# Gated scan and expert FFN kernel: the last second products by pairs of tiles, the last turned y over two banks, copies and turned states on finer signals

## The chip, the cores and the metric

The kernel runs on one core of one Trainium2 chip. The metric is the device time in microseconds (us) of one execution, as the median of several runs. Engines are TensorE (PE in the profile), VectorE (DVE), ScalarE (ACT), GpSimd (POOL) and SyncE (SP), which here only issues the DMAs.

## The reference, cut to what matters

Two sequences (batches) of 2048 tokens, 256 channels, all in f32. Every batch passes a recurrent layer and then a feed-forward layer, each between layer norms and added to what came in:

```
x = x + layernorm(attn(layernorm(x)))        # 512 inner channels, 32 heads of 16
x = x + layernorm(ffn(layernorm(x)))         # 2 of 8 experts, 1024 wide
# attn, for every token t, head by head, a state of two components S0, S1:
#   r0 = A11 S0 + A12 S1 ;  r1 = -A12 S0 + A11 S1
#   err = v - sum(k * r) ;  S = r + beta * err * k ;  y = sum(Q * S)
#   y = groupnorm(y, 32 groups, over tokens and channels of the group)
#   y = y * silu(z) + D * u ;  residual + y @ out_W.T
# ffn: pooled = mean of tokens; the best two experts by pooled @ Wr, weights by softmax
#   h = gelu(x @ W1[e] + b1[e]) ;  out = sum over the two e of w[e] * (h @ W2[e] + b2[e])
```

## The kernel before, in words

The code is written by hand for each engine as one program in order, with counting semaphores between them. No scheduler moves anything.

**Tiling.** The 2048 tokens of a batch are 128 chunks of 16 (L = 16). Partition c holds chunk c, and tile j holds token j of every chunk, so one step over j works on all chunks at once. The recurrence runs in two passes. `pass_1` finds for each chunk the map from its first state to its last. `chunk_scan` joins the 128 maps: VectorE multiplies the three parts of each component o by the end factors (L1733, L1734, `end_ready`), TensorE turns the results over (L624, `end_turned`), ScalarE copies the six turned parts into `mts` (L1030, `mt_ready`), VectorE scans them by small products (L1753 to L1774, `scan_done`), TensorE turns the chunks' first states back (L634, `start_ready`). `mts` lies where the first products of VectorE still read `PSt` (both are `work[0:3072]`), so that a copy may only begin when these are read.

**Pass 2** goes over j again: VectorE copies the turned states (L1798), rotates the queries of a tile by its coefficients (`turn`, L1784, after TensorE's query of L654), and does the updates of L1806 to L1825. After a tile, TensorE turns y_j into channel order (`turn_y`, L645, bank 6 or 7 of PSUM by j % 2), and ScalarE copies it out with its sum and squares it with its sum (L1047, L1052). After the last one VectorE takes the group sums (L1832), and the first gate (L1870) waits for the first normed y of ScalarE (L1082) and for x, which SP reloads once VectorE has finished the last tile.

**Experts.** Each batch's FFN has 64 units (NF). A unit is `up`, four instructions of 128x512 (L767) into bank 4 or 5, a gelu by ScalarE (L1158), and `down`, eight instructions of 128x256 (L781) that add to four token tiles in banks 6 and 7. 16 units complete a block of four tiles (two experts by eight). The FFN of batch 0 is spread through batch 1's recurrence in the code. That of batch 1 stands alone at the end. There the order on TensorE is up(i), down(i-1). Weights come by pairs of units into a ring of four pairs (`load_pairs`, L386 and L388), and pair p is issued when `down` of pair p-4 is finished. Behind the last pair in SP's queue stand the four stores of the result (L478). `last_norm` on VectorE takes each block: bias (L1992), statistics (L1272), moments (L1278 to L1284), with ScalarE's root (L1173), then scales (L2001), normed tiles (L2006) and sums with x1 (L2010).

The functions that the change touches, with the line numbers of the profile:

## Time and profile before

| what | value |
|---|---|
| median of 3 runs | 1417.45 us (1414.99 to 1418.44) |
| the profiled execution, its own time | 1417.05 us |
| its span | 1415.1 us |
| TensorE busy | 1248.4 us (88%) |
| VectorE busy | 1126.5 us (80%) |
| ScalarE busy | 794.4 us (56%) |
| GpSimd busy | 174.0 us (12%) |
| mean granted TensorE clock | 0.958 |

The span goes from the first to the last instruction of the profiled execution, and its own time lies 1.95 us above it. Busy shares are averages over stages that have different limits, so they do not tell which engine sets the end in a stage: in the recurrence VectorE is nearly always at work, in the last FFN TensorE is. The kernel writes two results to memory. The last of them leaves in four stores of 512 KB, and the span ends with the last one's landing.

### The profile page before, as it was taken

To read this page: it belongs to the slowest core of one execution; us is meant where nothing else is said; L and a number is where in the kernel's file an instruction comes from. 1 tells how busy PE (TensorE), PEld (TensorE's weight loads), DVE (VectorE), ACT (ScalarE), POOL (GpSimd) and SP (SyncE) were. 2 spreads that over 40 slices of the span, in tenths; PEclk is the share of its full clock that TensorE was granted. 3 is DMA by queue.
4 is the path that set the end of the run, shared out by engine and by line. 5 is a ranking of instruction groups with operands and counts; after the bars stand their busy time and mean duration, and the time that the engine had idled before them with its cause. 6 is when DMAs were issued, how large, how long until landed. Compare 5 with 4: busy or idle time off the path is not lost. (4 is left out here: it accounts for less than half of the span.)

```text
span 1415.1 us, 14617 instructions
## 1 busy us (share of the span) xinstructions
PE 1248.4 (88%) x4248; PEld 737.3 (52%) x4248; DVE 1126.5 (80%) x1826; ACT 794.4 (56%) x2713; POOL 174.0 (12%) x77
## 2 busy tenths in 40 slices
PE   5987788863999879798999999899998898999997
PEld 3553333332555446465565555555554565666664
DVE  5989999998999979789899999889999793411011
ACT  4896566623788866858322323347888565333232
POOL 0000155410122200000011111002221000000000
PEclk9999899986999999899999999999999898999999
DMA  6004111010311022501223131313110106232221
GB/s 238 1 8 179 60 57 48 30 59 1 119 45 60 30 110 83 223 23 45 89 90 104 61 104 60 104 60 119 56 49 31 60 1 219 74 135 75 75 75 74
DMA packets 54400, 110.88 MB, mean 78 GB/s; under 512 B 4785, under 2 KB 40114, under 8 KB 52274
## 3 DMA queue, kind: packets, MB, share of 16 engines
q1 hardware_dynamic: 54322, 109.97, 21.9%
q8 instruction: 34, 0.56, 0.2%
q14 instruction: 44, 0.36, 0.1%
HBM read 81.64 MB, written 28.31 MB: 78 GB/s over the span
## 5 line engine op out<-in xcount | busy, mean ns | idle before, releaser
L781 PE MATMUL ps<-kz 128*128 128x256 f32 x1024 | 243.5, 381 | 13.5 <-ACT kz L1158 8.8
L781 PEld LDWEIGHTS ps<-kz 128*128 128x128 f32 x1024 | 194.3, 191 | 97.0 <-issue 63.0
L767 PE MATMUL ps<-kz 128*128 128x512 f32 x512 | 241.0, 594 | 0.3 <-DVE small L1980 0.3
L1158 ACT ACTIVATE kz<-ps,small 128x512 f32<-128x512 f32 x128 | 87.7, 686 | 272.3 <-PE ps L767 272.1
L654 PE MATMUL ps<-wshare,uT 128*128 128x512 f32 x512 | 229.0, 601 | 5.3 <-DVE work L1784 5.2
L654 PEld LDWEIGHTS ps<-wshare,uT 128*128 128x128 f32 x512 | 96.2, 193 | 117.9 <-issue 109.4
L568 PE MATMUL ps<-wshare,xnT 128*128 128x512 f32 x256 | 120.8, 616 | 32.4 <-ACT ps L862 32.4
L1005 ACT ACTIVATE work<-ps,coef 128x16 f32<-128x16 f32 x736 | 124.4, 388 | 35.5 <-DVE work L1774 26.9
L1223 POOL TENSOR_TENSOR work<-work 128x1024 f32<-128x1024 f32 x28 | 66.9, 2391 | 582.7 <-DVE work L1692 354.6
L767 PEld LDWEIGHTS ps<-kz 128*128 128x128 f32 x512 | 97.2, 191 | 76.3 <-issue 70.2
L1992 DVE TENSOR_TENSOR kz<-ps,b_s 128x256 f32<-128x256 f32 x16 | 6.3, 414 | 135.9 <-PE ps L781 135.9
L1240 POOL TENSOR_TENSOR kz<-work 128x1024 f32<-128x1024 f32 x30 | 71.6, 2385 | 278.5 <-DVE work L1813 278.5
L568 PEld LDWEIGHTS ps<-wshare,xnT 128*128 128x128 f32 x256 | 47.7, 196 | 85.9 <-issue 48.7
L862 ACT ACTIVATE ps<-bk_s 128x1024 f32<-128x1024 f32 x32 | 32.9, 1029 | 101.5 <-DVE wshare L1600 101.5
L1005 ACT ACTIVATE wshare<-ps,coef 128x16 f32<-128x16 f32 x512 | 86.8, 405 | 2.0 <-DVE work L1823 2.0
L548 PE MATMUL ps<-wshare,uT 128*128 128x352 f32 x256 | 78.1, 467 | 4.5 <-ACT uT L936 2.8
L645 PEld LDWEIGHTS ps<-ident,kz 128*128 128x128 f32 x512 | 65.3, 201 | 27.7 <-DVE kz L1795 18.0
L645 PE MATMUL ps<-ident,kz 128*128 128x128 f32 x512 | 66.7, 286 | 10.7 <-DVE kz L1795 10.7
L1784 DVE TENSOR_TENSOR work<-ps,coef 128x1024 f32<-128x1024 f32 x60 | 70.5, 1218 | 1.4 <-PE ps L654 1.4
L716 PE MATMUL ps<-wo_s,work 128*128 128x256 f32 x256 | 61.0, 401 | 6.5 <-DVE work L1257 6.5
L548 PEld LDWEIGHTS ps<-wshare,uT 128*128 128x128 f32 x256 | 49.3, 194 | 33.2 <-issue 7.6
L693 PE MATMUL ps<-xnT,wz_s 128*128 128x512 f32 x128 | 60.1, 616 | 2.1 <-DVE work L1784 1.9
(293 smaller groups left out, 2099.6 us busy)
## 6 DMA issues: line engine op xcount, KB each, us to landing
kz<-in_w SPq DMA_DIRECT2D x128, 256.0 KB, 3.0
kap_d<-kz SPq DMA_DIRECT2D x26, 512.0 KB, 2.7
kz<-kap_d SPq DMA_DIRECT2D x26, 512.0 KB, 3.3
kz<-in_x SPq DMA_DIRECT2D x3, 2048.0 KB, 8.3
v_d<-kz SPq DMA_DIRECT2D x4, 1024.0 KB, 4.5
wshare<-in_wq SPq DMA_DIRECT2D x2, 2048.0 KB, 8.0
coef<-in_x SPq DMA_DIRECT2D x2, 2048.0 KB, 8.1
work<-v_d SPq DMA_DIRECT2D x3, 1024.0 KB, 7.5
```

The costliest lines, as they stand in the source:

```text
L548: t = mm(ps[:, sm_bank(b, j), 0:NSM * H], uT3[:, k, j * P:(j + 1) * P], wsm_s[:, k, :], start=(k == 0), stop=(k == KI - 1))
L568: t = mm(ps[:, k_bank(b, i) + c, :], xnT[:, k, j * P:(j + 1) * P], wk_s[:, k, c, :], start=False, stop=(k == KM - 1), skip_group_check=True)
L645: t = mm(ps[:, 6 + j % 2, g * P:(g + 1) * P], qb(j)[:, i, g * P:(g + 1) * P], ident[:], start=(i == 0), stop=(i == 1))
L654: t = mm(ps[:, 2 * (j % 2) + c, :], uT3[:, k, j * P:(j + 1) * P], wq_s[:, k, c, :], start=(k == 0), stop=(k == KI - 1))
L716: t = mm(ps[:, 4 + j % 4, 0:DM], y2(n)[:, g, q * P:(q + 1) * P], wo_s[:, g, :], start=(g == 0), stop=(g == KI - 1))
L767: t = mm(ps[:, 4 + i % 2, :], w1_r[r][:, k, (f % 2) * P:(f % 2 + 1) * P], x2T[:, k, n * 512:(n + 1) * 512], start=(k == 0), stop=(k == KM ...
L781: t = mm(ps[:, 6 + q // 2, (q % 2) * DM:(q % 2 + 1) * DM], hbuf(i)[:, q * P:(q + 1) * P], w2_r[r][:, f % 2, :], start=(f == 0 and q % 2 == ...
L1005: t = af(dst[:, h * HD:(h + 1) * HD], src[:, h * HD:(h + 1) * HD], ACT.Copy, scale=c[:, h:h + 1])
L1158: af(hbuf(i), ps[:, 4 + i % 2, :], ACT.Gelu, bias=b1_s[:, f // FT, f % FT:f % FT + 1]).then_inc(h_done, 1)
L1223: nc.gpsimd.tensor_tensor(PSt[:, :, 2], PSt[:, :, 2], Z, ALU.add).then_inc(sum_ready, 1)
L1240: nc.gpsimd.tensor_tensor(qb(j), w[0], w[1], ALU.add).then_inc(turned_ready, 1)
L1784: t = tt(w, q, wide(cf[:, H_ + i:H_ + i + 3:2, j]), MUL)
```

## The change

It does five things.

- **Last eight units by pairs of tiles.** In batch 1's FFN, the `up` of units 56 to 63 follow each other. Then come the `down` of all eight for the first two tiles (bank 6, `pair_done` 1), and of all eight for the last two (bank 7, `pair_done` 2). The gelus of the last four units go to `wshare`.
- **The last block's norm** is done by two tiles at a time (`last_block`). ScalarE norms three of the four tiles in place of VectorE. The last store is cut into two of 256 KB.
- **The last turned y** (j = 15) of each batch is written to banks 6 and 7, two groups in each, with a signal after the first two (`first_half`).
- **The scan's copies** wait for `parts_used` (after VectorE's product for o = 1, a = 0) for the first three, and for the second `end_ready` for the last three.
- **Batch 1's turned chunk states**: TensorE turns them after the first half of query 0 instead of after the whole, and VectorE rotates query 0 by halves, the first ahead of the state copy (`turn_half`).

```diff
@@ -294,6 +301,9 @@
+        def y_bank(j, g):
+            return 6 + (g // 2 if j == L - 1 else j % 2)
         def sm_bank(b, j):
@@ -313,7 +323,9 @@
-        def hbuf(i):
+        def hbuf(b, i):
+            if b == B - 1 and i >= NF - 4:
+                return wshare[:, (i - NF + 4) * 512:(i - NF + 5) * 512]
             return hid[:, (i % 4) * 512:(i % 4 + 1) * 512]
@@ -473,11 +485,12 @@
             load_pairs(B - 1, chosen, 14, NF // 2)
-            for n in range(NCH):
-                sp.wait_ge(out_ready, B - 1 + 4 * n + 4)
-                sp.dma_start(out[B - 1].rearrange("(c j) d -> c j d", j=L)[:, 4 * n:4 * n + 4], x1_tok[:, 4 * n:4 * n + 4]
+            stores = [(4 * n, 4 * n + 4) for n in range(NCH - 1)] + [(L - 4, L - 2), (L - 2, L)]
+            for r0, r1 in stores:
+                sp.wait_ge(out_ready, B - 1 + r1)
+                sp.dma_start(out[B - 1].rearrange("(c j) d -> c j d", j=L)[:, r0:r1], x1_tok[:, r0:r1]
                              ).then_inc(out_stored, 16)
-            sp.wait_ge(out_stored, 16 * (B - 1 + NCH))
+            sp.wait_ge(out_stored, 16 * (B - 1 + len(stores)))
@@ -636,24 +649,31 @@
                 pe.wait_ge(yp_ready, b * L + j + 1)
-                if j >= 2:
+                if j == L - 1:
+                    pe.wait_ge(yt_done, b * L + j)
+                elif j >= 2:
                     pe.wait_ge(yt_done, b * L + j - 1)
...
                 for g in range(KI):
+                    if j == L - 1 and g == 2:
+                        t.then_inc(first_half, 1)
                     for i in range(2):
-                        t = mm(ps[:, 6 + j % 2, g * P:(g + 1) * P], qb(j)[:, i, g * P:(g + 1) * P], ident[:],
+                        t = mm(ps[:, y_bank(j, g), g * P:(g + 1) * P], qb(j)[:, i, g * P:(g + 1) * P], ident[:],
                                start=(i == 0), stop=(i == 1))
                 t.then_inc(yt_ready, 1)
+            def query_part(j, c):
+                for k in range(KI):
+                    t = mm(ps[:, 2 * (j % 2) + c, :], uT3[:, k, j * P:(j + 1) * P], wq_s[:, k, c, :],
+                           start=(k == 0), stop=(k == KI - 1))
+                return t
...
                     pe.wait_ge(kq_used, 2 * L * b + L + j - 1)
-                for c in range(2):
-                    for k in range(KI):
-                        t = mm(ps[:, 2 * (j % 2) + c, :], uT3[:, k, j * P:(j + 1) * P], wq_s[:, k, c, :],
-                               start=(k == 0), stop=(k == KI - 1))
-                t.then_inc(kq_ready, 1)
+                query_part(j, 0)
+                query_part(j, 1).then_inc(kq_ready, 1)
@@ -666,10 +686,12 @@
                         token_u(b, L + j, j)
-                    if b > 0 or j > 2:
+                    if b > 0 and j == 0:
+                        query_part(0, 0).then_inc(half_query, 1)
+                        turn_starts(b)
+                        query_part(0, 1).then_inc(kq_ready, 1)
+                    elif b > 0 or j > 2:
                         query(b, j)
-                    if b > 0 and j == 0:
-                        turn_starts(b)
                     if j >= 3:
@@ -778,17 +800,31 @@
                     for q in range(4):
-                        t = mm(ps[:, 6 + q // 2, (q % 2) * DM:(q % 2 + 1) * DM], hbuf(i)[:, q * P:(q + 1) * P],
+                        t = mm(ps[:, 6 + q // 2, (q % 2) * DM:(q % 2 + 1) * DM], hbuf(b, i)[:, q * P:(q + 1) * P],
                                w2_r[r][:, f % 2, :], start=(f == 0 and q % 2 == 0), stop=(f == 2 * FT - 1),
+                def last_downs():
+                    for a in range(2):
+                        for i in range(NF - HELD, NF):
+                            r, f = i // 2 % WR, i % (2 * FT)
+                            if a == 0:
+                                pe.wait_ge(h_done, b * NF + i + 1)
+                                pe.wait_ge(w2s_ready, b * (NF // 2) + i // 2 + 1)
+                            for q in (2 * a, 2 * a + 1):
+                                t = mm(ps[:, 6 + a, (q % 2) * DM:(q % 2 + 1) * DM], hbuf(b, i)[:, q * P:(q + 1) * P],
+                                       w2_r[r][:, f % 2, :], start=False, stop=(i == NF - 1), skip_group_check=True)
+                        t.then_inc(pair_done, 1)
                 for i in range(first, last):
                     up(i)
-                    if i >= 1:
+                    if i >= 1 and (b < B - 1 or i <= NF - HELD):
                         down(i - 1)
-                if last == NF:
+                if last == NF and b < B - 1:
                     down(NF - 1)
+                elif last == NF:
+                    last_downs()
@@ -1023,8 +1059,10 @@
-                act.wait_ge(end_ready, b * 2 + 2)
+                act.wait_ge(parts_used, b + 1)
                 for o in range(2):
+                    if o:
+                        act.wait_ge(end_ready, b * 2 + 2)
                     for i in range(3):
@@ -1042,13 +1080,18 @@
                         silu(b, 6)
-                    act.wait_ge(yt_ready, b * L + j + 1)
+                    if j == L - 1:
+                        act.wait_ge(first_half, b + 1)
+                    else:
+                        act.wait_ge(yt_ready, b * L + j + 1)
                     for g in range(KI):
-                        t = af(y_tok[:, j, g * P:(g + 1) * P], ps[:, 6 + j % 2, g * P:(g + 1) * P], ACT.Copy,
+                        if j == L - 1 and g == 2:
+                            act.wait_ge(yt_ready, b * L + j + 1)
+                        t = af(y_tok[:, j, g * P:(g + 1) * P], ps[:, y_bank(j, g), g * P:(g + 1) * P], ACT.Copy,
                                accum_out=gs[:, g, 0, j:j + 1])
...
                     for g in range(KI):
-                        y = ps[:, 6 + j % 2, g * P:(g + 1) * P]
+                        y = ps[:, y_bank(j, g), g * P:(g + 1) * P]
                         t = af(y, y, ACT.Square, accum_out=gs[:, g, 1, j:j + 1])
@@ -1153,9 +1196,9 @@
                     act.wait_ge(h_ready, b * NF + i + 1)
-                    if i >= 4:
+                    if 4 <= i < NF - 4 or (i >= 4 and b < B - 1):
                         act.wait_ge(d_done, b * NF + i - 3)
-                    af(hbuf(i), ps[:, 4 + i % 2, :], ACT.Gelu, bias=b1_s[:, f // FT, f % FT:f % FT + 1]
+                    af(hbuf(b, i), ps[:, 4 + i % 2, :], ACT.Gelu, bias=b1_s[:, f // FT, f % FT:f % FT + 1]
                        ).then_inc(h_done, 1)
@@ -1166,7 +1209,14 @@
                 elif last == NF:
-                    block_root(NCH - 1)
+                    for a in range(2):
+                        r = slice(L - 4 + 2 * a, L - 2 + 2 * a)
+                        act.wait_ge(fin_vec, B + NCH - 1 + a)
+                        af(t1[:, r], mv[:, r, 1], ACT.Sqrt, bias=eps5).then_inc(fin_act, 1)
+                        act.wait_ge(fin_scale, a + 1)
+                        for j in range(L - 4 + 3 * a, L - 2 + 2 * a):
+                            t = af(r_tok[:, j], r_tok[:, j], ACT.Identity, scale=rs2[:, j:j + 1], bias=nb[:, j:j + 1])
+                        t.then_inc(fin_normed, 1)
@@ -1730,7 +1780,12 @@
                     for a in range(2):
-                        link(tt(by_head(X[:, a], 1), by_head(PSt[:, a], 1), wide(ef[:, o, a]), MUL))
+                        t = tt(by_head(X[:, a], 1), by_head(PSt[:, a], 1), wide(ef[:, o, a]), MUL)
+                        if o == 1 and a == 0:
+                            t.then_inc(parts_used, 1)
+                            dve.wait_ge(parts_used, b + 1)
+                        else:
+                            link(t)
                     tt(X[:, 0], X[:, 0], X[:, 1], ADD).then_inc(end_ready, 1)
@@ -1784,6 +1839,12 @@
+            def turn_half(b, c):
+                for i in range(2):
+                    t = tt(by_head(q_parts(b, 0)[i][:, c * DI:(c + 1) * DI], 0), by_head(ps[:, c, :], 0),
+                           wide(cf[:, H_ + i + 2 * c, 0]), MUL)
+                return t
             def pass_2(b):
@@ -1794,10 +1855,14 @@
+                if b > 0:
+                    dve.wait_ge(half_query, b)
+                    turn_half(b, 0)
                 dve.wait_ge(start_ready, b + 1)
...
                 if b > 0:
-                    turn(b, 0)
+                    dve.wait_ge(kq_ready, 2 * L * b + L + 1)
+                    turn_half(b, 1).then_inc(kq_used, 1)
                 dve.wait_ge(start_used, b + 1)
@@ -2008,6 +2073,42 @@
                             tt(x1_tok[:, j], r_tok[:, j], x1_tok[:, j], ADD).then_inc(out_ready, 1)
+            def last_block(b):
+                b2c = b2_s[:, 0]
+                def sums(a):
+                    dve.wait_ge(pair_done, a + 1)
+                    for q in (2 * a, 2 * a + 1):
+                        tt(r_tok[:, L - 4 + q], ps[:, 6 + a, (q % 2) * DM:(q % 2 + 1) * DM], b2c, ADD).then_inc(fd_used, 1)
+                    for q in (2 * a, 2 * a + 1):
+                        dve.wait_ge(fd_used, L - 4 + q + 1)
+                        seen = stats(L - 4 + q, r_tok[:, L - 4 + q])
+                    moments(seen, slice(L - 4 + 2 * a, L - 2 + 2 * a)).then_inc(fin_vec, 1)
+                def scales(a):
+                    r = slice(L - 4 + 2 * a, L - 2 + 2 * a)
+                    dve.wait_ge(fin_vec, b + NCH + a)
+                    dve.wait_ge(fin_act, b + NCH + a)
+                    link(v.reciprocal(rs2[:, r], t1[:, r]))
+                    stt(nb[:, r], mv[:, r, 0], -1.0, rs2[:, r], MUL, MUL).then_inc(fin_scale, 1)
+                def result(j):
+                    tt(x1_tok[:, j], r_tok[:, j], x1_tok[:, j], ADD).then_inc(out_ready, 1)
+                sums(0)
+                scales(0)
+                sums(1)
+                dve.wait_ge(fin_normed, 1)
+                result(L - 4)
+                result(L - 3)
+                scales(1)
+                dve.wait_ge(fin_scale, 2)
+                t = mark(tsc(r_tok[:, L - 2], r_tok[:, L - 2], rs2[:, L - 2:L - 1], nb[:, L - 2:L - 1], MUL, ADD))
+                after(t)
+                result(L - 2)
+                dve.wait_ge(fin_normed, 2)
+                result(L - 1)
```

**ScalarE at batch 1's scan.** L1030 (after: L1068) are the six copies. L1158 (after: L1201) are the gelus around them. Before:

```order
L1154 ACTIVATE kz<-kz,small 128x512 [waits w_loaded0]
L1158 ACTIVATE kz<-ps,small 128x512 [waits d_done,h_ready]
L1030 ACTIVATE work<-ps 128x64x8 [waits end_turned,end_ready]
L1030 ACTIVATE work<-ps 128x64x8 [waits end_turned] x5
L1158 ACTIVATE kz<-ps,small 128x512 [waits d_done,h_ready]
L1154 ACTIVATE kz<-kz,small 128x512 [waits w_loaded1]
```

The first copy waited for the second `end_ready`, and with it all six and the gelu behind them. Of the change:

```order
L1197 ACTIVATE kz<-kz,small 128x512 [waits w_loaded0]
L1201 ACTIVATE kz<-ps,small 128x512 [waits d_done,h_ready]
L1068 ACTIVATE work<-ps 128x64x8 [waits end_turned,parts_used]
L1068 ACTIVATE work<-ps 128x64x8 [waits end_turned] x2
L1068 ACTIVATE work<-ps 128x64x8 [waits end_turned,end_ready]
L1068 ACTIVATE work<-ps 128x64x8 [waits end_turned] x2
L1201 ACTIVATE kz<-ps,small 128x512 [waits d_done,h_ready]
```

The order is the same. Only the wait for the second `end_ready` has moved from the first copy to the fourth.

**TensorE at the end of the program.** L767 (after: L789) is `up`, L781 is `down` (after: L816 in the held part). Before:

```order
L767 MATMUL ps<-kz 128x512 [waits h_done,w_loaded3]
L767 MATMUL ps<-kz 128x512
L781 MATMUL ps<-kz 128x256 [waits w2s_ready,h_done]
L781 MATMUL ps<-kz 128x256 x3
L781 MATMUL ps<-kz 128x256 [waits w2s_ready,h_done]
L781 MATMUL ps<-kz 128x256 x3
L43 UNCONDITIONAL_BRANCH
```

All four tiles got their last products in the last rows. Of the change, from the last `up` (the last `down` for the first pair of tiles and all of the second pair):

```order
L789 MATMUL ps<-kz 128x512 [waits h_done,w_loaded3]
L789 MATMUL ps<-kz 128x512
L816 MATMUL ps<-kz 128x256 [waits w2s_ready,h_done]
L816 MATMUL ps<-kz 128x256
```
```order
L816 MATMUL ps<-kz,wshare 128x256 [waits w2s_ready,h_done]
L816 MATMUL ps<-kz,wshare 128x256
L816 MATMUL ps<-kz 128x256 x8
L816 MATMUL ps<-kz,wshare 128x256 x8
L44 UNCONDITIONAL_BRANCH
```

The eight `down` of two products each for the first pair have their waits. The sixteen products of the second pair (x8 and x8) stand behind them and wait for nothing.

**VectorE at the end of the program**, from the last moments. Before:

```order
L1257 SCALAR_TENSOR_TENSOR small<-small 128x4 [waits vec_chain]
L2001 RECIPROCAL small<-small 128x4 [waits fin_act,fin_vec]
L1257 SCALAR_TENSOR_TENSOR small<-small 128x4 [waits vec_chain]
L2006 TENSOR_SCALAR kz<-kz,small 128x256 [waits vec_chain]
L2006 TENSOR_SCALAR kz<-kz,small 128x256
L2010 TENSOR_TENSOR coef<-kz,coef 128x256 [waits vec_chain]
L2006 TENSOR_SCALAR kz<-kz,small 128x256
L2010 TENSOR_TENSOR coef<-kz,coef 128x256 [waits vec_chain]
L2006 TENSOR_SCALAR kz<-kz,small 128x256
L2010 TENSOR_TENSOR coef<-kz,coef 128x256 [waits vec_chain] x2
```

Of the change:

```order
L2083 TENSOR_TENSOR kz<-ps,b_s 128x256 [waits pair_done]
L2083 TENSOR_TENSOR kz<-ps,b_s 128x256
L1322 BN_STATS small<-kz 128x6 [waits fd_used] x2
```
```order
L1307 SCALAR_TENSOR_TENSOR small<-small 128x2 [waits vec_chain]
L2097 TENSOR_TENSOR coef<-kz,coef 128x256 [waits fin_normed]
L2097 TENSOR_TENSOR coef<-kz,coef 128x256
L2093 RECIPROCAL small<-small 128x2 [waits fin_act,fin_vec]
L1307 SCALAR_TENSOR_TENSOR small<-small 128x2 [waits vec_chain]
L2107 TENSOR_SCALAR kz<-kz,small 128x256 [waits fin_scale]
L2097 TENSOR_TENSOR coef<-kz,coef 128x256 [waits vec_chain]
L2097 TENSOR_TENSOR coef<-kz,coef 128x256 [waits fin_normed]
```

After the last product there are two tiles of bias and statistics instead of four, and one tile normed by VectorE instead of four. The sums of the first pair of tiles stand ahead of the last reciprocal.

## Rows read from the trace of the kernel before

**Rows 1.** Busy time by stretch: us of PE, PEld, DVE, ACT, POOL, then PEclk, DMA share, GB/s.
```profile
965.00:1095.00 130.00, 122.43 (x472) 70.01 (x470) 128.18 (x133) 113.77 (x660) 30.62 (x13) 0.99 0.19 65
1186.00:1405.00 219.00, 217.32 (x759) 143.59 (x758) 42.66 (x146) 75.01 (x107) 0.00 (x0) 1.00 0.31 108
```

**Rows 2.** Timeline (start, us, engine, line, operation), batch 1's scan: DVE, ACT, PE.
```profile
901.67 3.55 DVE L1733 TENSOR_TENSOR work<-work,endf 128x1536 f32<-128x1536 f32 x2
912.51 1.03 DVE L1753 TENSOR_TENSOR work<-work 128x384 f32<-128x384 f32 x2 [5.17 <-ACT work L1030]
907.05 5.43 ACT L1030 ACTIVATE work<-ps 128x512 f32<-128x512 f32 x6 [8.07 <-DVE work L1734]
...
907.07 0.65 PE L624 MATMUL ps<-ident,work 128*128 128x128 f32 x4 [0.34 <-DVE work L1734]
912.99 1.99 PE L781 MATMUL ps<-kz 128*128 128x256 f32 x8 [1.58 <-ACT kz L1158]
```

**Rows 3.** Timeline, batch 1's first queries and turned states: PE, then DVE.
```profile
934.20 7.03 PE L654 MATMUL ps<-wshare,uT 128*128 128x512 f32 x16
941.07 1.04 PE L634 MATMUL ps<-ident,work 128*128 128x128 f32 x8
942.38 7.03 PE L654 MATMUL ps<-wshare,uT 128*128 128x512 f32 x16
...
935.37 1.78 DVE L1774 TENSOR_TENSOR work<-work 128x896 f32<-128x896 f32 x1
942.14 1.23 DVE L1798 COPY work<-ps 128x1024 f32<-128x1024 f32 x1 [4.08 <-PE ps L634]
949.45 2.36 DVE L1784 TENSOR_TENSOR work<-ps,coef 128x1024 f32<-128x1024 f32 x2 [1.36 <-PE ps L654]
```

**Rows 4.** Timeline of DVE at batch 0's scan.
```profile
308.43 3.55 DVE L1733 TENSOR_TENSOR work<-work,endf 128x1536 f32<-128x1536 f32 x2
...
314.08 4.62 DVE L1784 TENSOR_TENSOR kz<-ps,coef 128x1024 f32<-128x1024 f32 x4
319.30 1.03 DVE L1753 TENSOR_TENSOR work<-work 128x384 f32<-128x384 f32 x2 [0.61 <-ACT work L1030]
```

**Rows 5.** Timeline, last turned y: PE, ACT (third copy), DVE of batch 1; DVE of batch 0.
```profile
1105.23 1.95 PE L645 MATMUL ps<-ident,kz 128*128 128x128 f32 x16
...
1107.74 0.28 ACT L1047 ACTIVATE kz<-ps 128x128 f32<-128x128 f32 x1
...
1113.34 1.33 DVE L1870 TENSOR_TENSOR work<-kz,wshare 128x512 f32<-128x512 f32 x2 [0.95 <-ACT kz L1082]
...
513.77 1.29 DVE L1870 TENSOR_TENSOR work<-kz,wshare 128x512 f32<-128x512 f32 x2 [1.06 <-DMA coef<-in_x]
```

**Rows 6.** Timeline of the end, with SP's queue (SPq), and the last stretch by engine.
```profile
1380.24 32.23 SPq L478 DMA_DIRECT2D out<-coef  x4
1401.48 3.62 PE L781 MATMUL ps<-kz 128*128 128x256 f32 x16
1405.14 0.76 DVE L1992 TENSOR_TENSOR kz<-ps,b_s 128x256 f32<-128x256 f32 x2 [39.24 <-PE ps L781]
1408.57 0.30 ACT L1173 ACTIVATE small<-small 128x4 f32<-128x4 f32 x1 [4.90 <-DVE small L1257]
1411.35 0.76 DVE L2010 TENSOR_TENSOR coef<-kz,coef 128x256 f32<-128x256 f32 x2
...
1413.00:1414.00 1.00, 0.00 (x0) 0.00 (x0) 0.00 (x0) 0.00 (x0) 0.00 (x0) 0.50 0.98 401
```

**Rows 7.** Line L388, second weight load of a pair: issue to landing over all 64.
```profile
DMA to landing us min/median/max: 2.8/3.0/10.9
```

**Rows 8.** Timeline of PE, the output product of two blocks of batch 1 and one of batch 0.
```profile
1118.96 10.03 PE L716 MATMUL ps<-wo_s,work 128*128 128x256 f32 x32 [3.20 <-DVE work L1257]
...
1132.27 7.07 PE L716 MATMUL ps<-wo_s,work 128*128 128x256 f32 x32
...
519.36 8.86 PE L716 MATMUL ps<-wo_s,work 128*128 128x256 f32 x32 [3.27 <-DVE work L1257]
```

10 lines of the change are left out of this document (9 added, 1 removed).

## The prediction, made before the changed kernel had run

> **What bounds the kernel now.** I read the busy time by stretch first, because the change touches stages with different limits. In batch 1's second pass VectorE is at work for 128.18 of 130 us, in the last FFN TensorE for 217.32 of 219 us at a granted clock of 1.00 [rows 1]. So what VectorE gets earlier ahead of a second pass should last to its end, and the last FFN can only be shortened behind its last product. Then I read the timelines of the places that the change touches, for the idle time in brackets and what ended it. There the reader should see which of two waits ends last, since only that one is worth anything. Each term below is measured in the profiled execution, 1417.05 us of its own time, span 1415.1. The median of the runs shown is 1417.45, 0.4 above it.
>
> **1. The scan's copies, batch 1.** The six copies of ScalarE start at 907.05, when VectorE has finished all products and sums, and take 5.43 us, 0.905 each. VectorE idles 5.17 us for them and goes on at 912.51. TensorE's `down` at 912.99 waits for the gelu that stands behind them [rows 2]. Now the first three wait for the third product only. VectorE's pair of products from 901.67 takes 3.55, so the first of it ends at 903.45. Three copies end at 906.2, ahead of the second `end_ready` at 907.03. The fourth waits for four turning instructions from 907.07, 0.65 long [rows 2]: 907.75, and three copies end at 910.47. That is 2.0 us before the 912.48 at which they end now. New waits: behind `parts_used` on ScalarE stand the copies and the gelu, which came later before. On VectorE it takes the place of a wait for the same product, at no cost. TensorE's waits for `mt_ready` are then met early. The gelu moves by the same 2.0, and with it TensorE's seven `down` and five `up` before the queries. Gain for VectorE and TensorE: 2.0 us.
>
> **2. Halved query, batch 1.** Before, TensorE runs without a gap from query 0 (934.20, ended 941.07) over the turned states (to 941.94) to query 1, whose last product ends at 949.41. VectorE gets the states at 942.14 after 4.08 us idle, but then waits another 1.36 us for query 1, until 949.45 [rows 3]. The last wait here is TensorE's sum of work, and the change only reorders it. With term 1, half of query 0 ends at 934.20 - 2.0 + 3.44 = 935.64, turned states at 936.51, the other half at 939.95, query 1 at 947.4. The scan ends at 935.37 + 1.78 - 2.0 = 935.15, so TensorE's wait for it, with the half query and query 1 now queued behind, costs nothing by 0.5 us. If that slack fails, it costs at most what the scan is late: 1.5 us if the copies did nothing for VectorE. VectorE's half turns of 512 columns from PSUM have no row. They lie between the 256 columns of L1992 (0.38 each) and the 1024 of L1784 (1.18 each) [rows 3, 6]. I take 0.6. The first two run from 936.1 to 937.3, the copy to 938.5, and the second two wait for 939.95 with the whole pass queued behind them, and end at 941.2. The next tile's first work (2.6 us before) ends near 943.9, and VectorE waits 3.5 us for query 1 at 947.4 instead of 1.36. So VectorE is 4 us early at one place and 2.0 early at the next. Worth of this edit by itself: 0 (from -0.3 to +0.2). Terms 1 and 2: 2.0 us, from 0.5 to 2.1.
>
> **3. The scan's copies, batch 0.** They gain the same 2.0 there, but VectorE turns two queries meanwhile: four L1784 from 314.08, 4.62 long, to 318.70. It then idles only 0.61 before 319.30 [rows 4]. Gain 0.6 us, from 0 to 0.6.
>
> **4. The last turned y.** TensorE's 16 instructions take 1.95 us from 1105.23 in batch 1, and ScalarE then copies and squares with a copy each 0.25 us. The third copy starts at 1107.74 [rows 5]. With two banks the first two copies run while TensorE fills bank 7, and the third starts when it has ended, at 1107.22. Gain 0.5 at the copies, and at the sums behind them. New waits: TensorE waits for the squares of tile 14 instead of tile 13, which ScalarE has finished some 3 us before 1105.23, and behind it stands a gate tile for which ScalarE has no use until the normed y. In batch 1 the first gate waits for ScalarE's normed y and gets the 0.5. In batch 0 the same gate waits 1.06 us for the reload of x [rows 5], a DMA that is issued when VectorE ends the last tile and does not move with this edit. Gain 0 there. Sum 0.4, from 0 to 0.5.
>
> **5. The end.** TensorE's order changes, its work does not: 32 instructions of `up` and 64 of `down`. So it ends at 1405.10 as before [rows 6], if the eight `up` do not stall. They wait for the gelu two units back (0.2 + 0.69 us against an `up` of 1.72), and for the last weight pair. Its DMAs stand in SP's queue ahead of the stores that go out at 1380.24 [rows 6]; the usual landing is 3.0 us [rows 7]. It was needed at 1398 and is now needed after `down` 55 (1379.27) and five `up`: 1387.9. That leaves over 7 us for 3.0. The first pair of tiles has its last product at 1398.2, so its bias, statistics, root and norm, and ScalarE's table load, lie beside the second pair's 6.9 us.
>
> Behind the last product VectorE needs, before, from 1405.14 to 1412.11: 6.97 us [rows 6]. Of that, eight tile operations at a step of 0.33 (two in 0.76) are 2.73, and moments the rest to the root at 1408.57, 0.66. Now: four tile operations 1.41, moments 0.66, two sums of the first pair 0.7 (the root's round trip of 0.44 runs beside them, so the place of these sums costs 0.3), scales 0.4, one normed tile 0.45, two sums 0.75. That is 4.4 us, a gain of 2.6. ScalarE norms the last tile meanwhile: 256 columns, between the 0.28 of 128 columns [rows 5] and the 0.905 of a 512-column copy [rows 2]. I take 0.55. It stays hidden under VectorE's tile and sum (0.8), and at 0.9 costs 0.1. The last store is 256 KB instead of 512: at 401 GB/s [rows 6] 1.3 us become 0.65. The other half is issued 1.5 us earlier and is gone by then. Gain 0.6, from 0.3. Term 5: 3.2 us, from 2.2 to 3.5.
>
> **Sum.** 2.0 + 0.6 + 0.4 + 3.2 = 6.2 us. The profiled execution would come to 1410.85, the median to 1411.2. With all low ends the gain is 2.7, with all high ones 6.7.
>
> **The rivals.** *A: the middle gives nothing that lasts.* Two of its terms depend on slacks of half a microsecond or less (TensorE's wait for the scan, the reload of x in batch 1), and a DMA or a wait that the timeline does not show could hold the next stage. For it speaks batch 0, where a DMA already eats term 4. Against it speaks the second pass with under 2 us of idle in 130 [rows 1]. Then only term 5 is left: 1417.45 - 3.2 = 1414.2.
>
> *B: the last pair lands late.* It shares the DMA engines with three stores of 512 KB from 1380.24. The longest landing of such a load is 10.9 us [rows 7]. The pair would be there at 1390.7, and TensorE would stall 2.8 us at the seventh `up`: 1414.0. It decides from a landing of 8 us. Against it: the weights stand ahead of the stores.
>
> *C, the slow side: the clock in the output products.* The first 32 products of batch 1's output, behind a pause of 3.20 us, take 10.03 us, the 32 of the next block 7.07. In batch 0 the first 32 take 8.86 [rows 8]. So the trace pays 3.0 and 1.8 us for a granted clock that is at 1.2 GHz in a part of them, and how long that part is differs between two batches with the same pause. The change moves what comes before these products by fractions of a microsecond. If the level were low through both blocks of 32, each would take about 14.1: 4.1 and 5.2 us more than now, 9.3 in all. Less 6.2, the kernel is 3.1 us slower: 1420.5. It decides against the change once two thirds of that is lost. It may as well give back up to 4.8. For it: such stretches exist and lie on the path. Against: it was high again before the end in both.
>
> The rule behind this one is in the Trainium skill, "TensorE: Matmul & The Clock Gate", Part 1: the gate is not in step with the program, so that one kernel can start with a different number of slow matmuls from run to run. The 10.03 against 8.86 behind equal pauses agrees [rows 8]. By that rule C is not caused by the change and comes and goes between runs, so a median would hold little of it. By the rows alone it could be fixed by the new timing.
>
> **How the numbers follow.** The sum holds: 0.71, with its own range of 1409.3 to 1413. A: 0.16. B: 0.05. C: 0.08, of which a part only cancels the gain. Predicted 1411.2. The range to hold 8 in 10 takes in A and B and a gain from the clock: 1408.8 to 1414.5. A measurement of this kernel tells 0.3%, 4.25 us, from no change, so "faster" means under 1413.2. The sum lies there (0.70 of its 0.71), and a bit of A and B with two terms still alive (0.04): 0.74. A, B and the mild C give "the same", 0.21. The rest of C is "slower", 0.05.
>
> **What would show it.** In batch 1, VectorE's first scan product starts 5.2 - 2.0 = 3.2 us after its last memset instead of 5.2, and TensorE's wait before the `down` is gone by the same. The states' copy comes some 4 to 5 us early, but the second tile's turn only 2.0 early, behind an idle of about 3.5 us on TensorE. In batch 0 the idle of 0.61 is nearly gone. The third copy of y comes 0.5 early, and the first gate of batch 0 waits longer for the reload. At the end, TensorE's eight `up` stand without a gap, its last product ends as long after the last FFN's begin as before, VectorE needs 4.4 us behind it, and the span ends about 2.4 us after the last sum. I would be wrong if TensorE idles between 1379 and 1405 (shifted), if the time between the two second passes' ends and the next stage grows, or if the output products' first blocks take over 12 us.

## The result, and the profile after

| | before | after |
|---|---|---|
| median, first comparison (6 runs each) | 1416.51 us | 1407.01 us |
| all runs of the same two programs, over three comparisons | 1416.25 (50 runs, 1412.3 to 1418.6) | 1407.95 (18 runs, 1405.0 to 1412.7) |
| profiled execution, span | 1415.1 us | 1404.5 us |
| mean granted TensorE clock | 0.958 | 0.963 |
| TensorE busy | 1248.4 us | 1243.3 us |

The ratio is 0.9934, 95% interval 0.9921 to 0.9947: 9.5 us in the first comparison, 8.3 over all runs. I had reckoned 6.2 and predicted 1411.2 us, so the kernel is faster than the range of 1408.8 to 1414.5 us held. The profiled execution gained 10.6 us of span.

The profile of after follows in the order of [rows 2 to 8]. Columns are start, us, engine, line, operation, and in brackets the idle time ahead and what ended it. Batch 1's scan and first queries, first ScalarE, then VectorE, then TensorE:

```profile
903.03 2.90 ACT L1068 ACTIVATE work<-ps 128x512 f32<-128x512 f32 x3 [4.48 <-DVE work L1783]
907.39 2.81 ACT L1068 ACTIVATE work<-ps 128x512 f32<-128x512 f32 x3 [1.46 <-PE ps L637]
...
910.23 1.03 DVE L1808 TENSOR_TENSOR work<-work 128x384 f32<-128x384 f32 x2 [3.32 <-ACT work L1068]
935.68 1.28 DVE L1844 TENSOR_TENSOR work<-ps,coef 128x512 f32<-128x512 f32 x2
936.88 1.21 DVE L1862 COPY work<-ps 128x1024 f32<-128x1024 f32 x1
939.86 1.29 DVE L1844 TENSOR_TENSOR work<-ps,coef 128x512 f32<-128x512 f32 x2 [1.77 <-PE ps L668]
947.17 2.35 DVE L1839 TENSOR_TENSOR work<-ps,coef 128x1024 f32<-128x1024 f32 x2 [3.56 <-PE ps L668]
...
931.92 3.60 PE L668 MATMUL ps<-wshare,uT 128*128 128x512 f32 x8
935.35 1.04 PE L647 MATMUL ps<-ident,work 128*128 128x128 f32 x8
936.23 3.60 PE L668 MATMUL ps<-wshare,uT 128*128 128x512 f32 x8
```

VectorE's idle time ahead of the scan fell from 5.17 [rows 2] to 3.32 us. The state copy comes 5.3 us early (942.14 [rows 3] to 936.88), and the second tile's turn only 2.28 (949.45 to 947.17), behind 3.56 us of idle. Of the 2.28, 0.43 were there before the scan (901.67 [rows 2] to 901.23).

The group sums behind the last turned y of batch 1 and the first gate, both on VectorE. Then, all on TensorE, the first 32 output products of batch 0 (518.11) and of batch 1 (1115.96) and two groups of eight of batch 1's mean over the tokens:

```profile
1106.67 0.28 DVE L1897 TENSOR_REDUCE small<-small 128x8 f32<-128x128 f32 x1 [4.11 <-ACT ps L1095]
1110.37 1.29 DVE L1935 TENSOR_TENSOR work<-kz,wshare 128x512 f32<-128x512 f32 x2 [1.03 <-DMA coef<-in_x]
...
518.11 9.89 PE L738 MATMUL ps<-wo_s,work 128*128 128x256 f32 x32 [3.35 <-DVE work L1307]
1115.96 7.17 PE L738 MATMUL ps<-wo_s,work 128*128 128x256 f32 x32 [3.24 <-DVE work L1307]
1158.96 3.34 PE L747 MATMUL ps<-coef,small 128*1 128x256 f32 x8 [2.98 <-DVE small L1307]
1163.78 1.89 PE L747 MATMUL ps<-coef,small 128*1 128x256 f32 x8 [1.48 <-DVE small L1307]
```

The gate came 2.97 us early (1113.34 [rows 5] to 1110.37). The 32 products behind it took 7.17 us where before took 10.03 [rows 8], and those of batch 0 took 9.89 where before took 8.86. The same two groups of batch 1's mean in before:

```profile
1164.83 2.71 PE L725 MATMUL ps<-coef,small 128*1 128x256 f32 x8 [2.99 <-DVE small L1257]
1169.66 3.31 PE L725 MATMUL ps<-coef,small 128*1 128x256 f32 x8 [2.11 <-DVE small L1257]
```

That is the clock. The stretch of ten microseconds under batch 1's products in before, then in after (us; busy time of PE, PEld, DVE, ACT, POOL; granted clock; DMA share; GB/s):

```profile
1119.00:1129.00 10.00, 10.00 (x33) 8.29 (x34) 6.99 (x13) 4.66 (x7) 0.00 (x0) 0.71 0.01 2
```
```profile
1116.00:1126.00 10.00, 10.00 (x40) 7.50 (x41) 9.49 (x24) 5.70 (x9) 0.00 (x0) 1.00 0.01 2
```

TensorE is busy for the whole of both. A mean of 0.71 says that a part of the stretch ran at 1.2 GHz, and TensorE did 33 instructions there, where it did 40 at 2.4 GHz. The end of after:

```profile
1390.73 3.62 PE L816 MATMUL ps<-kz 128*128 128x256 f32 x16
1394.18 3.62 PE L816 MATMUL ps<-kz,wshare 128*128 128x256 f32 x16
...
1397.84 0.76 DVE L2083 TENSOR_TENSOR kz<-ps,b_s 128x256 f32<-128x256 f32 x2 [4.05 <-PE ps L816]
1400.89 0.41 DVE L2107 TENSOR_SCALAR kz<-kz,small 128x256 f32<-128x256 f32 x1
1401.33 0.76 DVE L2097 TENSOR_TENSOR coef<-kz,coef 128x256 f32<-128x256 f32 x2
...
1400.88 0.60 ACT L1218 ACTIVATE kz<-kz,small 128x256 f32<-128x256 f32 x1 [0.65 <-DVE small L1307]
```

VectorE needs 4.25 us behind the last product (1397.84 to 1402.09), where it needed 6.97.

### The profile page after: what moved, and what is told of

The parts are those of the page before. It is cut to its first block and busy times, and to the rows that moved or that the text cites. A ratio compares the mean times of both kernels' runs of the same rounds, so it can differ in the third digit from the quotient of the medians.

```text
span 1404.5 us, 14628 instructions
## 1 busy us (share of the span) xinstructions
PE 1243.3 (89%) x4248; PEld 735.3 (52%) x4248; DVE 1126.0 (80%) x1833; ACT 793.2 (56%) x2717; POOL 173.9 (12%) x77
## 5 line engine op out<-in xcount | busy, mean ns | idle before, releaser
L789 PE MATMUL ps<-kz 128*128 128x512 f32 x512 | 240.1, 594 | 0.3 <-DVE small L2045 0.3
L803 PE MATMUL ps<-kz 128*128 128x256 f32 x960 | 228.6, 381 | 12.7 <-ACT kz L1201 8.0
L1201 ACT ACTIVATE kz<-ps,small 128x512 f32<-128x512 f32 x124 | 84.7, 684 | 259.4 <-PE ps L789 259.1
L803 PEld LDWEIGHTS ps<-kz 128*128 128x128 f32 x960 | 182.1, 191 | 91.6 <-issue 59.6
L789 PEld LDWEIGHTS ps<-kz 128*128 128x128 f32 x512 | 97.3, 191 | 78.8 <-issue 73.1
L1090 ACT ACTIVATE kz<-ps 128x128 f32<-128x128 f32 x128 | 33.6, 277 | 49.4 <-PE ps L662 49.4
```

The source lines that it names most:

```text
L789: t = mm(ps[:, 4 + i % 2, :], w1_r[r][:, k, (f % 2) * P:(f % 2 + 1) * P], x2T[:, k, n * 512:(n + 1) * 512], start=(k == 0), stop=(k == KM ...
L803: t = mm(ps[:, 6 + q // 2, (q % 2) * DM:(q % 2 + 1) * DM], hbuf(b, i)[:, q * P:(q + 1) * P], w2_r[r][:, f % 2, :], start=(f == 0 and q % 2 ...
L1201: af(hbuf(b, i), ps[:, 4 + i % 2, :], ACT.Gelu, bias=b1_s[:, f // FT, f % FT:f % FT + 1]).then_inc(h_done, 1)
```

## The experiments

The numbers are the median, its ratio to before with the 95% interval, and lengths read from the trace. "Products" are the first 32 output products of a batch. They take 7.17 us where the clock is 2.4 GHz throughout.

**The end alone** (`last_block`, `last_downs`, the split store; all else as before).

```diff
+                elif last == NF:
+                    last_downs()
```


> The kernel before with the end of the change alone (last eight units by pairs of tiles, last block's norm by two tiles, five stores). Theory S (the parts give what was reckoned, and what came on top is TensorE's granted clock in batch 1's output and mean products, which goes with the middle edits): 3.3 us under the kernel before, the ratio 0.9977, first 32 output products of batch 1 still near 10 us. Rival T (the extra gain belongs to the end, by a faster last FFN): 6 us or more, ratio 0.9957 or less.

Measured: 1414.1 us (9 runs), 0.9975 [0.9965, 0.9985]. From TensorE's end to the span's end it gains 3.3 us. No instruction ahead of the last FFN is changed, and the products take 8.86 and 10.13 us, as they do in before. Theory S came out, and term 5 is right.

**All but the end.**

```diff
-                elif last == NF:
-                    last_downs()
```


> The change without its end: copies, halved query with turned states, last turned y over two banks. Theory S: 3.2 us from the parts and about 3 to 4 us from the clock, 6 to 7 in all, ratio 0.9953, batch 1's first 32 output products at 7.2 us as in the changed kernel, since all that stands ahead of them is the same. Rival T: 3.2 us, ratio 0.9977, whatever these products take. Rival R (the clock there is chance of a run): the products take anything between 7 and 14 us, and the time does not repeat from run to run.

Measured: 1408.47 us (4 runs), 0.9938 [0.9921, 0.9954], 8.8 us under before, where terms 1 to 4 are 3.0. Products 7.17 and 8.86. In this trace the clock gave 1.7 and 1.2 us in the products and 1.4 in batch 0's mean. Another 1.1 us of its span lie ahead of batch 0's scan, where its code is that of after (first scan product at 317.30 against 318.41). So the missing part lies in the middle of the program. Theory S failed in one point: it had batch 1's products at 7.2 us, because all that stands ahead of them is the same as in after, and they took 8.86. And the two halves of the change give 3.2 and 8.8 us, 12.0 together, where the whole gave 9.5. Fixed gains of the two parts would add up.

**The scan's copies alone**, and **the last turned y alone**.

```diff
-                act.wait_ge(end_ready, b * 2 + 2)
+                act.wait_ge(parts_used, b + 1)
                 for o in range(2):
+                    if o:
+                        act.wait_ge(end_ready, b * 2 + 2)
```


> The scan's copies on their finer signals alone. By the sum 2.0 us in batch 1 and 0.6 in batch 0: 2.6, ratio 0.9982, if the clock in the products behind stays as before. The clock may move it by up to 3 us either way, since it shifts batch 1's output products by about 2.6 us; the profile tells by the length of their first 32 (10.0 before, 7.2 in the changed kernel). If the copies did not carry the middle's gain, VectorE's first scan product in batch 1 would still come 5.2 us after its memset.

Measured: 1409.61 us (4 runs), 0.9944 [0.9927, 0.996]. Products 7.17 and 8.58. The 7.7 us are more than the expected 2.6 and 3 from the clock on top.

```diff
+                    if j == L - 1:
+                        act.wait_ge(first_half, b + 1)
```


> The last turned y over two banks alone. By the sum 0.4 us (batch 1 only, since in batch 0 the first gate waits for the reload of x): ratio 0.9997. It shortens TensorE's pause ahead of the group sums from 1.25 to about 0.7 us, so if that pause is what sets the clock in the output products behind it, their first 32 would fall to 7.2 us with this edit alone and the kernel gain about 3 us more, ratio 0.9976. If only the moment at which they start matters, they may stay at 10.

Measured: 1413.09 us (9 runs, 1410.0 to 1414.8), 0.9973 [0.9962, 0.9983]. Products 7.17 and 10.11. Two edits with direct terms of 2.6 and 0.4 us gave 7.0 and 3.8 us of span. Their directly touched steps moved by about what was reckoned (0.8 and 1.9 us at the two scans, 0.5 at the group sums), and most of the rest lies where the products or the mean run faster. Both get the same 1.7 us in batch 0's products, with a start 0.7 us earlier. The second edit cut TensorE's pause ahead of the group sums' product from 1.25 to 0.72 us, and batch 1's products stayed at 10.11: that pause is not what sets them.

**Query 0 not halved** (the rest of the change kept).

```diff
-                    if b > 0 and j == 0:
-                        query_part(0, 0).then_inc(half_query, 1)
-                        turn_starts(b)
-                        query_part(0, 1).then_inc(kq_ready, 1)
```


> The changed kernel without the halved query: query 0 whole, then the turned states, then the copy and the whole turn, as before. By the sum the edit is worth 0 (-0.3 to +0.2), since TensorE's work up to query 1 sets the end there: VectorE's turn for the second tile starts at the same time as in the changed kernel (2.28 us ahead of the kernel before), behind an idle of about 1.4 us instead of 3.56. Time as the changed kernel, 1407.0, ratio 0.9934. If the halves matter, it is 1 to 2 us slower.

Measured: 1407.33 us (4 runs), 0.9946 [0.9924, 0.9967]. The second tile's turn stands at 947.38 against 947.17, with the whole query turned at once behind the state copy. This edit is worth 0.2 us at most, as expected.

**TensorE kept at work in the pauses.** Extra products whose results nobody reads stand ahead of each batch's first output product (3) and of the mean's second and third groups (3 and 2). Such a product is two instructions in the trace and takes 0.86 us. Once on the kernel before, once on the changed one.

```diff
+                    if n == 0:
+                        fill(4, 3)
                     pe.wait_ge(y2_ready, b * NV + (n + 1) * KI)
...
+                    if j in (8, 12):
+                        fill(0, 3 if j == 8 else 2)
```


> The kernel before with extra products on TensorE, whose results nobody reads, in its pauses ahead of the output products (three pairs of 128x512) and of the mean products for tile 8 (three pairs) and tile 12 (two pairs), in both batches. Theory S (the extra gain is the granted clock in these stretches, which stays high if TensorE does not pause ahead of them): batch 1's first 32 output products take 7.1 us instead of 10.0, batch 0's 7.1 instead of 8.9, the mean products' slow part goes. 3.0 + 1.8 + about 1.4 + 1.4, some 6 to 7 us less than the kernel before, ratio 0.9953, with not one instruction of the path removed. Rival P (the clock in them is set by something other than the pause): lengths and time as before or a little above.

> The changed kernel with the same extra products. Theory S: its batch 0 pays 2.8 us in the output products (9.9 against 7.1) and about 1.4 in the mean products, its batch 1 almost nothing, so it gains some 4 us, to about 1403, ratio to the kernel before 0.990. Against the filled kernel before it is then faster by the parts' own sum alone, 6.2 us, and no longer by 9.5. If that difference stays at 9 us, the parts themselves give more than was reckoned and the clock is not the cause.

Measured: 1409.77 us (4 runs), 0.9954 [0.9938, 0.9971] on before, 1407.9 (4 runs, 1401.7 to 1409.0), 0.993 [0.9903, 0.9958] on after. All products take 7.17 us and both groups 1.89. The products of batch 0 and 1 in the filled kernel before:

```profile
519.79 7.17 PE L722 MATMUL ps<-wo_s,work 128*128 128x256 f32 x32 [0.62 <-DVE work L1265]
1116.16 7.17 PE L722 MATMUL ps<-wo_s,work 128*128 128x256 f32 x32 [0.62 <-DVE work L1265]
```

So some 6.5 us of the kernel before are a low clock in these stretches. Of the changed kernel I expected 6.2 us under the other, and got 1.9. Its trace shows the clock low further on, in batch 0's turning and first routed products (L797, eight instructions, 3.70 us at 2.4 GHz), and once more in batch 0's experts (L811, a `down` that takes 1.97 at this place in after):

```profile
571.35 2.40 PE L768 MATMUL ps<-ident,kz 128*128 128x128 f32 x12 [0.86 <-ACT kz L1183]
574.46 2.79 PE L768 MATMUL ps<-ident,kz 128*128 128x128 f32 x12 [0.72 <-ACT kz L1183]
578.09 5.74 PE L797 MATMUL ps<-kz 128*128 128x512 f32 x8 [0.32 <-DVE small L2053]
...
787.90 3.75 PE L811 MATMUL ps<-kz 128*128 128x256 f32 x8 [2.97 <-ACT kz L1191]
```

From the turning to the end of the routed products it takes 3.3 us more than the filled kernel before. From the `down` to batch 1's scan it takes 123.83 us, where the kernels with the new copies and a high clock there take 122.2: 1.6 more. Together that is 4.9 us, and 4.3 were missing. Both are low clocks that this run had and its partner had not. One of its four runs took 1401.73 us.

**The group sums of batch 1 held up**, by 4 and by 8 small chained memsets on VectorE (0.53 us for the four, 1.13 for the eight).

```diff
+                if b == 1:
+                    for _ in range(8):
+                        link(v.memset(small[:, 520:544], 0.0))
```


> The changed kernel with four chained settings of 24 unused columns on VectorE ahead of batch 1's group sums, about 0.8 us in all. Nothing else moves ahead of the output products. If the moment at which TensorE pauses and starts decides the clock there, their first 32 take longer than the 7.2 us of the changed kernel, up to 10, or stay if 0.8 us is too little to reach the next step of the clock. If the changed instructions themselves decide it, they stay at 7.2 and the kernel loses 0.8 us.

> The changed kernel with eight small memsets of a dead column stretch on VectorE ahead of batch 1's group sums, each chained to the next: they hold the group sums, the gate and the first output product up by about 1.2 us (four took 0.6 us). Theory (which clock the output products get is a matter of when they start): the 32 products take a length between 7.17 and 10.1 us that need not be 7.17, so the loss at the end of the program is 1.2 us plus anything from 0 to 2.9 us, and with the mean products anything from -0.5 to 4.5 us altogether: time 1408 to 1411.5. Rival (only the direct terms count and the products' length is set by the code): products 7.17 again, mean 3.34 and 1.89 again, and the time 1407.0 + 1.2 = 1408.2.

Measured, one run each: 1405.56 and 1409.41 us. Products of batch 1 took 8.86 and 7.17, those of batch 0 7.17 and 9.89, though nothing had been changed in batch 0. That spoiled the comparison of two delays. The 7.17 behind the eight memsets is no test of a later start either: the clock was low in the twelve gate instructions ahead (7.09 us instead of 5.40), so that TensorE paused 1.50 us there and not 3.2. What the two runs do show stands in batch 0: identical code gets different lengths in different runs.

**The two programs again**, nothing edited.

> The changed kernel once more, nothing edited: a second profile of the same program. Theory (the gain over the reckoned 6.2 us is TensorE's granted clock in batch 1's output products and mean products, and that clock's steps stand at moments that differ by tenths of a microsecond from run to run): the median lies within 1.5 us of 1407.0; in its profile the steps that the change touches directly stand where they stood in the first profile within 0.3 us (batch 1's scan 1.9 us shorter, the end 3.3 us shorter), while the lengths of the first 32 output products (9.89 and 7.17 us) and of the 8-product groups of the mean (1.89 to 3.3 us) are free to come out differently. Rival (the same program always gets the same clock at the same place, so that these lengths belong to the code): 9.89, 7.17, 2.85, 3.25, 3.34 and 1.89 us again within 0.1 each.

> The changed kernel a third time, nothing edited. Theory (a draw of the clock): the median between 1407 and 1410, the distance to before between 6.5 and 9.5; the first 32 output products of batch 0, which have started within 0.2 us of 518.15 in four profiles of kernels with this code before them, take 9.9 us again (9.9 to 10.1), since they start at the same moment within 0.2 us, while batch 1's, whose start has moved by 0.5 us between the first two profiles, take anything from 7.17 to 10.1. Rival (the first set's 1407.0 was the change and the second set's 1410.0 a disturbance of that chip): 1407.0 within 0.5 and batch 1's products 7.17 again.

> The kernel before, nothing edited, for a second profile of it. Theory (its own trace was a dear draw that mostly repeats, since nothing moves its starts): the 32 products of batch 0 and of batch 1 again between 8.8 and 10.2 us, the mean's groups again 2.6 to 3.4, the median 1416 to 1417.5. Rival (the lengths of a trace are chance even with nothing moved): at least one of the two stretches of products comes out at 7.17.

Measured: the changed kernel 1409.96 us (6 runs, 1405.4 to 1412.0), 0.995 [0.9934, 0.9966], and 1407.45 (6 runs, 1405.0 to 1412.7), 0.9938 [0.9922, 0.9953]; the kernel before 1415.99 (10 runs), 0.9998 [0.9989, 1.0007]. The same products in the second profile of after:

```profile
518.22 9.90 PE L738 MATMUL ps<-wo_s,work 128*128 128x256 f32 x32 [3.30 <-DVE work L1307]
1116.44 8.86 PE L738 MATMUL ps<-wo_s,work 128*128 128x256 f32 x32 [3.35 <-DVE work L1307]
1161.12 2.68 PE L747 MATMUL ps<-coef,small 128*1 128x256 f32 x8 [2.97 <-DVE small L1307]
1165.94 3.33 PE L747 MATMUL ps<-coef,small 128*1 128x256 f32 x8 [2.15 <-DVE small L1307]
```

The median of this set, 1409.96, is 3 us above the first and not within the expected 1.5. Batch 0's products and mean groups came out as in the first profile to 0.1 us, which was what the rival had. Batch 1's did not: its products took 1.69 us more, with a start 0.5 us later. The third profile repeats this (1116.58, 8.86; mean 2.60 and 3.37). The second profile of before, batch 0 and 1:

```profile
519.18 8.86 PE L716 MATMUL ps<-wo_s,work 128*128 128x256 f32 x32 [3.19 <-DVE work L1257]
1118.65 10.07 PE L716 MATMUL ps<-wo_s,work 128*128 128x256 f32 x32 [3.19 <-DVE work L1257]
```

It repeats the first. Starts and lengths of batch 0's products in all twelve profiles without extra products, in order of start:

| start, us | length, us | kernel |
|---|---|---|
| 517.12, 517.41 | 7.17, 7.17 | all but the end; 4 memsets |
| 518.05 to 518.25 (5 profiles) | 9.89 to 10.07 | after, three times; query not halved; 8 memsets |
| 518.64, 518.66 | 7.17, 7.17 | the copies alone; the last y alone |
| 519.18, 519.36, 520.37 | 8.86 each | before, twice; the end alone |

In batch 0 equal starts went with equal lengths, to 0.2 us, and the length is not monotone in the start. It is not tied to the code either: seven of the twelve have the same code up to here, and five of them took 9.89 to 10.07, two 7.17. In batch 1 even the start does not tell: 1116.40 (query not halved) gave 7.17 and 1116.44 (the second profile of after) 8.86, behind pauses of 3.47 and 3.35 us. So a start goes together with a length in one batch. It is not shown that it sets it. The starts themselves differ by 1 us between runs of the same code.

**Larger fills.** Two more extra products ahead of every second tile's turning in batch 0, from tile 6 on.

```diff
+                    if b == 0 and j >= 6 and j % 2 == 0:
+                        fill2(7, 2)
```


> The changed kernel with the extra TensorE products of the kernel filled_after (3 ahead of each batch's first output product, 3 and 2 ahead of the mean's second and third groups, results that nobody reads) and two more of them ahead of every second tile's turning in batch 0 from the seventh tile on, where filled_after's profile had the lower clock from 572.0 to 582.2 us and stood 3.4 us later at the first routed products' end than the filled kernel of before did. Theory (filled_after missed its 6.2 us against filled_before only because the lower clock came up there instead): the turning and the first routed products run at 2.4 GHz, that 3.4 us comes back, less about 0.5 us for fillers that overlap the pauses imperfectly: 1403.5 to 1406.5, and its distance to filled_more_before 4.5 to 7. Rival (the changed kernel loses elsewhere what fillers give it): 1407 to 1409, distance 1 to 3.

> The kernel before with the same extra products as filled_more_after. Its own profile with the first set of fillers had no lower clock in the turning, so theory: 1409.5 to 1411 (filled_before gave 1409.8, plus up to 0.8 us for ten more fillers of 0.2 us each that stand in pauses of 0.9 and 1.4 us). Rival: under 1408, were there lower-clock stretches in most runs that its one profile did not show.

Measured: 1409.56 us (6 runs), 0.9951 [0.9939, 0.9964], and 1416.09 (11 runs), 0.9993 [0.9984, 1.0001]. I had the extra products at 0.2 us each, and they are 0.86: they cost 6.7 us of path in the second kernel (batch 0's choice of experts ends at 584.04 instead of 577.31). Neither expected time came out. The distance did: 6.5 us between the medians.

**Fills that fit their pauses.** One ahead of tiles 4 and 10 of batch 0's turning, and two ahead of the wait for the experts' weights in batch 1.

```diff
+                    if b == 0 and j in (4, 10):
+                        fill2(7, 1)
...
                 turn_x2(b, 4, 8 if b == B - 1 else L)
+                if b == B - 1:
+                    fill2(7, 2)
```


> The changed kernel with filled_after's extra TensorE products (3, 3 and 2 per batch), and in the turning of batch 0 one more ahead of the fifth and of the eleventh tile, in batch 1 two ahead of the wait for the experts' weights, whose results nobody reads: each takes 0.86 us (a pair of them 1.88 us in the profile of filled_more_before), and the pauses there are 0.86, 0.7 to 1.4 and 2.2 us, so that they cost 0 to 0.5 us in all. Theory: the 3.4 us that filled_after lost between 572 and 582 us come back, and 0.7 us in batch 1's last turned rows: 1403.0 to 1406.0 and 5.5 to 7 below filled_light_before. Rival (a lower clock comes up in another stretch instead, as it did in filled_after): 1407 to 1409.

> The kernel before with the same extra products. Theory: filled_before gave 1409.8 without a lower clock in batch 0's turning, and batch 1's last turned rows gain up to 0.7 us: 1409 to 1411. Rival (the extra products delay the turned rows that they stand ahead of): 1411.5 or more.

Measured: 1402.64 us (4 runs, 1402.1 to 1404.0), 0.9901 [0.9886, 0.9915], and 1409.24 (5 runs, 1407.6 to 1410.3), 0.9947 [0.9934, 0.996]. The first time lies 0.4 us under the expected range. The distance is 6.6 us, as expected, and the first beats both kernels: 13.3 us under before. Its trace, at the mean and in the same turning and routed products:

```profile
1156.88 1.89 PE L759 MATMUL ps<-coef,small 128*1 128x256 f32 x8 [0.21 <-DVE small L1323]
1161.70 1.89 PE L759 MATMUL ps<-coef,small 128*1 128x256 f32 x8 [1.02 <-DVE small L1323]
...
571.13 1.71 PE L774 MATMUL ps<-ident,kz 128*128 128x128 f32 x12
574.12 1.82 PE L774 MATMUL ps<-ident,kz 128*128 128x128 f32 x12 [0.42 <-ACT kz L1191]
576.57 3.70 PE L805 MATMUL ps<-kz 128*128 128x512 f32 x8 [0.32 <-DVE small L2061]
...
1177.57 1.98 PE L805 MATMUL ps<-kz 128*128 128x512 f32 x4 [0.82 <-DMA kz<-in_w]
...
784.28 3.75 PE L819 MATMUL ps<-kz 128*128 128x256 f32 x8 [2.97 <-ACT kz L1199]
```

All but the last row are at 2.4 GHz, behind shorter pauses. What waits next there is a weight pair: 0.82 us. The last row is the `down` in batch 0's experts again, with the clock low. It took 3.75 us in four of the six kernels with extra products, among them both of this pair, and 1.97 in all twelve profiles without. So the low clock has left the stretches with extra products, and not the program.

## Why the prediction was wrong

The gain of the three profiled executions of after over the first of before, in us of span, cut at the same points of the program. The third is of a run that took 1410.81 us, 3.4 above the median of its set:

| stretch | reckoned | 1st | 2nd | 3rd |
|---|---|---|---|---|
| start to the end of batch 0's choice of experts | 0.6 | 0.32 | 0.19 | 0.04 |
| to batch 1's first scan product | 2.0 | 1.96 | 1.74 | 1.94 |
| to the first output product (terms 2 and 4) | 0.4 | 0.73 | 0.59 | 0.40 |
| batch 1's first 32 output products | 0 | 2.86 | 1.17 | 1.18 |
| to batch 1's first routed product | 0 | 1.49 | 0.02 | 0.00 |
| to the end of the span | 3.2 | 3.24 | 3.28 | 3.26 |
| sum | 6.2 | 10.6 | 7.0 | 6.8 |

The first row holds term 3 and what the clock did to batch 0's products.

- **Term 1, the copies of batch 1: right.** 2.0 predicted, 1.85 measured at the scan, and it lasted over the whole second pass.
- **Term 2, the halved query: right.** Worth 0 to 0.2 us.
- **Term 3, the copies of batch 0: right, then lost.** The state copy came 0.7 us early beyond the 0.2 before it (predicted 0.6), and up to the first output product 1.25 had come together. The products there took 1.03 more than before and left 0.22.
- **Term 4, the last turned y: right within 0.3.** The group sums came 0.75 us early in batch 1 instead of 0.5. The gate then had the reload of x as its last wait, also in batch 1 (1.03 us), so a little of it was lost.
- **Term 5, the end: right.** Tail 4.25 us against 4.4, no stall at the eight `up`, 3.3 us in all. Rival B did not happen, and neither did A: what the middle gave lasted to the first output product.
- **The step that failed** is the sum: it has no term for the clock. The low clock of the products was taken over for after as it stood in the trace of before, 3.0 and 1.8 us, and that of the mean was not looked at. Rival C had it as a loss of up to 9.3 or a gain "up to 4.8", at a chance of 0.08 together, and the range had room for half of that gain. This is the term that was mis-sized, at 0. It measured from 0 to 3.3 us net in three profiles of the same program (2.9 and 1.5 less the 1.0 of batch 0 in the first, 1.2 less about as much in the others), and over all runs about 2 (8.3 measured less 6.2). The trace of before was not an unusual run: its two profiled executions took 1417.05 and 1416.65 us, where the median of 50 is 1416.25. Its two profiles and the kernel with the end alone have the same code ahead of these products, which came out at 8.86 and 10.03 to 10.13 in all three. No trace of any kernel showed batch 1's longer than 10.13, and full clock is 7.17. So batch 1's stretch in before stood near its dear end, and there was more to win than to lose. With the middle changed, and no extra products, nine profiles have batch 1's products under 10 us in eight, and batch 0's shorter than before in four and longer in five.
- **The starting value** adds a little: 1411.2 was reckoned down from a median of 1417.45, and before took 1416.51 in the comparison. Of the 4.2 us between prediction and measurement 0.9 are that, and 3.3 the gain (9.5 less 6.2). The second comparison, with 1409.96 for the same program, would have fallen into the range. Where in the spread the first one fell is luck.

With the low clock filled away on both sides in these stretches, the change is worth 6.6 us (medians 1409.24 and 1402.64), and 6.5 with the larger fills. That is close to the reckoned 6.2, though not a clean measure of it: the first fills gave 1.9, and of the light pair the profiled executions lie 5.5 us of span apart, both with a low clock elsewhere. What the direct steps gave is read more safely where they stand: 1.85 us at batch 1's scan, 0.7 at batch 0's, 0.75 at the last turned y, 3.3 at the end.

That the rest changes from run to run (a draw, in the words of the expectations) is shown by the same program's lengths of 7.17, 8.86 and 8.86 in batch 1, and in batch 0 by two of seven profiles at 7.17, with the same code so far. The spread of after's runs, 7.7 us over 18 against 6.3 over 50, fits and proves little. What sets the moments at which the clock falls and rises stays open, and so does how large the gain is in the long run: the three comparisons gave 9.5, 7.3 and 8.5 us.

## What to carry to other kernels

Where a trace shows a matmul stretch at a low granted clock behind a pause, price it in a forecast as a range from the stretch at full clock to its dearest length in any batch, for before as well as after. If before sits near the dear end, as batch 1's products did here, the change has more to win than to lose there. Ask whether the pause can be filled before anything is shaved ahead of it: here fills that took no instruction off the path gave 6.7 us, as much as the change itself, and the runs of the light pair agree within 1.9 and 2.7 us. A fill has to fit its pause, by its measured length, and all pauses in reach have to be looked at, since the low clock can come up at another one, as it did at the turning and in batch 0's experts.

## What the hardware showed

- The same 32 products took 7.17, 8.58, 8.86 or 9.89 to 10.13 us. The Trainium skill says in "TensorE: Matmul & The Clock Gate", Part 1, that the gate is not in step with the program. The traces agree for batch 1 (7.17 and 8.86 in the same program). For batch 0 they show more order than that suggests: three profiles of one program gave 9.89, 9.90 and 10.04, and only two of seven with the same code so far gave something else, 7.17.
- Behind pauses of 3.2 to 3.6 us on TensorE, 17 of 23 stretches of these products had a low clock in them. With the pause cut to 0.6 to 0.9 us by extra products, all twelve stretches in the six kernels with them took 7.17 us. A short pause alone is no safeguard: the turning in the changed kernel with the first fills ran at a low clock behind pauses of 0.86 and 0.72 us.
- A product of 128x512 in f32 is two instructions in the trace. Two such products took 1.72 us from start to start at 2.4 GHz, 0.86 each.
- ScalarE's tile of 256 columns took 0.60 us, and VectorE's two half turns of 512 columns from PSUM 1.28, 0.64 each. I had taken 0.55 and 0.6.
